# Four-layer network in one kernel: block attention scored by halves, and the routed MLP of four batches moved into the last GLA stages

## What is computed

```python
logits = jnp.einsum('bhtqd,bhtknd->bhtqkn', Qb, Ksel).reshape(Bx, H, Tr, BM, k * BN) * scale
P = jax.nn.softmax(logits, axis=-1)
Ob = jnp.einsum('bhtqs,bhtsd->bhtqd', P, Vsel.reshape(Bx, H, Tr, k * BN, D))
```

```python
top1 = jnp.argmax(gate_probs, axis=-1)
masked = xf[None, :, :] * one_hot.T[:, :, None]
h = jax.nn.relu(jnp.einsum('end,edh->enh', masked, w1) + b1[:, None, :])
expert_out = jnp.einsum('enh,ehd->end', h, w2) + b2[:, None, :]
routing_output = expert_out.sum(axis=0)
shared = jax.nn.relu(xf @ sw1 + sb1) @ sw2 + sb2
return (routing_output + shared).reshape(B, S, D)
```

## Time and profile before

| what | value |
|---|---|
| median of 3 runs | 3938.86 us (3933.8 to 3939.21) |
| the profiled execution's own time | 3959.75 us |
| its span in the profile | 3958.0 us |
| PE, VectorE, ScalarE, GpSimd busy | 3376.5, 2329.6, 1704.5, 528.2 us |
| block attention, from the first exponential of unit 0 to that of unit 31 | 298.6 us |
| GLA stages 14, 15, 16, 17 | 75.17, 63.37, 71.40, 56.80 us |

### The profile page before, as it was taken

One profiled execution on the slowest core, in us unless ns is written; L12 is line 12 of the kernel. 1 busy time (PEld: TensorE's weight loads), 2 busy tenths in 40 slices (PEclk: granted clock), 3 DMA queues, 4 the chain that ended last, 5 costly groups with the idle time before them and its releaser, 6 DMA issues. The chain is left out here.

```text
span 3958.0 us, 124996 instructions
## 1 busy us (share of the span) xinstructions
PE 3376.5 (85%) x55256; PEld 2105.7 (53%) x55256; DVE 2329.6 (59%) x6280; ACT 1704.5 (43%) x3930; POOL 528.2 (13%) x532
## 2 busy tenths in 40 slices
PE   3875665689999999999886996999999999999985
PEld 1334553235555545555564443666666666666672
DVE  3766664267767667676882113666666656666545
ACT  1666774364444444344211434443434444434323
POOL 0212331000000000000000001222222222222210
PEclk9897777789989889898665997999999999999967
DMA  2000000221111111110000001000000000000000
GB/s 90 0 0 1 2 2 3 79 67 40 45 42 46 40 32 53 34 45 29 3 3 18 0 5 41 2 3 2 3 2 3 3 2 3 3 2 2 3 2 24
DMA packets 37036, 77.17 MB, mean 19 GB/s; under 512 B 7696, under 2 KB 11152, under 8 KB 35472
## 3 DMA queue, kind: packets, MB, share of 16 engines
q1 hardware_dynamic: 36496, 69.17, 5.5%
HBM read 64.83 MB, written 4.33 MB: 17 GB/s over the span
## 5 line engine op out<-in xcount | busy, mean ns | idle before, releaser
L1401 PE MATMUL ps<-g_hs,g_fc 128*128 128x512 f32 x448 | 271.6, 691 | 53.2 <-DVE g_hs L1715 37.9
L1523 ACT ACTIVATE g_hidden<-ps 128x512 f32<-128x512 f32 x224 | 133.1, 594 | 409.1 <-PE ps L1401 409.0
L1292 PEld LDWEIGHTS ps<-g_Q,g_K 32*32 32x32 f32 x12288 | 204.5, 120 | 182.3 <-issue 95.6
L2168 PE MATMUL ps<-d_hp,d_w_k 128*128 128x512 f32 x512 | 282.1, 637 | 0.0
L1292 PE MATMUL ps<-g_Q,g_K 32*32 32x32 f32 (+1 forms) x12288 | 235.7, 226 | 27.7 <-DVE g_H L1561 10.0
L1415 PE MATMUL ps<-g_hidden,g_proj 128*128 128x512 f32 x448 | 257.3, 662 | 0.0
L2246 POOL TENSOR_TENSOR d_sq<-d_QK 128x512 f32<-128x512 f32 x128 | 133.0, 1039 | 925.1 <-ACT d_QK L2297 763.8
L2266 ACT ACTIVATE d_F<-ps 128x128 f32<-128x128 f32 x256 | 70.8, 276 | 351.3 <-PE ps L2077 348.0
L778 ACT ACTIVATE att_p<-ps,att_mx 128x96 f32<-128x96 f32 x512 | 165.9, 361 | 70.1 <-DVE att_mx L723 64.5
L1260 POOL COPY g_xb<-X 128x512 f32<-128x512 f32 x8 | 7.2, 906 | 1209.8 <-DVE X L1721 1098.5
L2441 DVE SCALAR_TENSOR_TENSOR d_conv<-ps,w_conv_q,d_conv 128x511 f32<-128x511 f32 (+2 forms) x192 | 142.2, 741 | 33.9 <-ACT d_conv L2291 30.0
(11 more groups left out here) (478 smaller groups left out, 7895.1 us busy)
## 6 DMA issues: line engine op xcount, KB each, us to landing
g_hs<-gate_rows SPq DMA_DIRECT2D x56, 256.0 KB, 3.4
g_fc<-in_c_fc_dram SPq DMA_DIRECT2D x56, 256.0 KB, 4.0
g_proj<-in_c_proj_dram SPq DMA_DIRECT2D x56, 256.0 KB, 2.8
X<-in_x_dram SPq DMA_DIRECT2D x1, 2048.0 KB, 10.7
w_c_fc<-in_c_fc_dram SPq DMA_DIRECT2D x1, 2048.0 KB, 8.3
w_c_proj<-in_c_proj_dram SPq DMA_DIRECT2D x1, 2048.0 KB, 12.7
ex_root<-gate_rows SPq DMA_DIRECT2D x1, 2048.0 KB, 15.2
h_rows<-k SPq DMA_DIRECT2D x1, 2048.0 KB, 6.3
```

Source lines behind the costliest of these rows:

```text
L1292: ins = e.matmul(later(scored, n_), keys_, queries(n_, planes, r_, 4 * i + j), start=(turn_ == 0 and part == 0 and n_ != 1), stop=(part == 1),
L1401: e.matmul(P[2], fc[:, n % 2, ts(f, C)], hs[:, n % 2], start=True, stop=True).then_inc(pe.steps, pe.did(now(f"u{i}")))
L1523: e.activation(r[:, slot], P[2], ACT.Relu).then_inc(act.steps, act.did(now(f"r{i}")))
L2168: ins = e.matmul(b, w_k[:, j, ts(H, C)], hp_of(u)[:, j:j + T], start=(j == 0), stop=(j == TAPS - 1))
```

## The change

In the attention, `scores` and `maximum` get a half as a second argument. Scores of half 0 (banks 0 and 1, row groups 0 and 1) wait for ScalarE's exponentials of half 0 of the unit before instead of for all of them, and `maximum` of half 0 moves on VectorE ahead of `pick_heads(n - 1)` and of `weigh(n, 1)`. The PE issues both halves at the place where it issued the 16 matmuls.

In `gla`, stages 14 to 17 get `routed` = 0 to 3. There the pieces `up`, `down` and `residual` carry the routed MLP of batch 0 to 3, in buffers of the expert MLP. Its weights come by six transfers on SP at the end of stage 13. `up` 0, 1 and 3 are centre, mean and score, `up` 4 to 15 the 12 up matmuls, `down` 3 to 14 the 12 down matmuls. VectorE gets pieces `up` 2 (two instructions) and `up` 3 (two), and two in `residual`. `routed_mlp` then does batches 4 to 7. Three small weights are loaded at the start of the program, and not ahead of `routed_mlp`.

```diff
@@ block_attention
-                        e.wait_ge(pe.steps, pe.at(f"s{last_of(q - RING)}"))
+                        e.wait_ge(pe.steps, pe.at(f"s{last_of(q - RING)}1"))
...
-                def maximum(n):
+                def maximum(n, half):
                     if n >= 2:
-                        e.wait_ge(act.steps, act.at(f"exp{n - 2}3"))
-                    e.wait_ge(pe.steps, pe.at(f"s{n}"))
-                    for half in range(2):
-                        m4 = mx[:, n % 2, ts(half, 8)].rearrange("p (g n) -> p g n", g=2)
-                        e.tensor_reduce(m4, scored[:, ts(half, 2)], AX.X, ALU.max, negate=True).then_inc(dve.steps, dve.did(f"max{n}{half}"))
+                        e.wait_ge(act.steps, act.at(f"exp{n - 2}{2 * half + 1}"))
+                    e.wait_ge(pe.steps, pe.at(f"s{n}{half}"))
+                    m4 = mx[:, n % 2, ts(half, 8)].rearrange("p (g n) -> p g n", g=2)
+                    e.tensor_reduce(m4, scored[:, ts(half, 2)], AX.X, ALU.max, negate=True).then_inc(dve.steps, dve.did(f"max{n}{half}"))
...
                     weigh(n, 0)
+                    if n + 1 < UNITS:
+                        maximum(n + 1, 0)
                     if n:
                         pick_heads(n - 1)
                     weigh(n, 1)
                     if n + 1 < UNITS:
-                        maximum(n + 1)
+                        maximum(n + 1, 1)
                         keep_values(n + 1)
...
-                def scores(n):
+                def scores(n, half):
                     q, u = place_of(n)
                     e.wait_ge(dve.steps, dve.at(f"q{q}"))
                     if n:
-                        e.wait_ge(act.steps, act.at(f"exp{n - 1}3"))
+                        e.wait_ge(act.steps, act.at(f"exp{n - 1}{2 * half + 1}"))
                     for b in range(4):
-                        for g in range(4):
+                        for g in (2 * half, 2 * half + 1):
...
                     if n + 1 < UNITS:
-                        scores(n + 1)
+                        scores(n + 1, 0)
+                        scores(n + 1, 1)
@@ gla
+        routed_h, hidden_rows, masked = hx, r[:, 0:3], r[:, 3:5]
+        routed_up = {2: fc[:, 0], 0: fc[:, 1], 1: hs[:, 0]}
+        routed_down = {2: proj[:, 0], 0: proj[:, 1], 1: hs[:, 1].rearrange("p (f x) -> p f x", f=4)}
+        FEED = (2, 0, 1)
...
+            routed = n - 2 * (B - 1) if half is None and sg is not None else None
...
+                        if c["routed"] == 0:
+                            e.wait_ge(dve.steps, dve.at(was("residual")))
+                            for p_ in FEED:
+                                e.dma_start(routed_up[p_], a["w1_2"][:, p_, :]).then_inc(dma.steps, dma.did())
+                                e.dma_start(routed_down[p_], a["w2_2"][:, p_]).then_inc(dma.steps, dma.did(now("routed")))
...
+                    def routed_step(i):
...
+                        elif i == 3:
+                            e.wait_ge(dve.steps, dve.at(now("rh")))
+                            e.matmul(P[3], routed_gate[:], routed_h[:], start=True, stop=True).then_inc(pe.steps, pe.did(now("rscore")))
+                        elif i >= 4:
+                            x = i - 4
+                            p_, f = FEED[x // 4], x % 4
...
+                            if x:
+                                e.wait_ge(act.steps, act.at(now(f"rr{x - 1}")))
+                            if p_ < 2:
+                                e.wait_ge(dve.steps, dve.at(now(f"rm{p_}")))
+                            moving = routed_h[:] if p_ == 2 else masked[:, p_]
+                            e.matmul(P[2], routed_up[p_][:, ts(f, C)], moving, start=True, stop=True).then_inc(pe.steps, pe.did(now(f"ru{x}")))
+                    def routed_total(x):
...
+                        e.wait_ge(act.steps, act.at(now(f"rr{x}")))
+                        e.matmul(P[3], routed_down[FEED[x // 4]][:, x % 4, :], hidden_rows[:, x % 3], start=(x == 0), stop=(x == 11)).then_inc(pe.steps, pe.did(now(f"rd{x}")))
@@ routed_mlp
-        order = [(b, p_, f) for b in range(B) for p_ in (2, 0, 1) for f in range(4)]
+        order = [(b, p_, f) for b in range(B_LEFT) for p_ in (2, 0, 1) for f in range(4)]
@@ build
-                routed_mlp(k)
+                routed_mlp(k, 4)
```

More of the change, by code:

```diff
@@ L117 @@
 GROUPS = {
-    "all": ["center", "mean", "ident"],
+    "all": ["center", "mean", "ident", "gate_w2", "b1_2", "b2_2"],
     "modulation": ["cT", "wmod"],
@@ L751, in _ @@
                 gather_queries(0)
-                maximum(0)
+                maximum(0, 0)
+                maximum(0, 1)
                 keep_values(0)
@@ L1217, in in_turn @@
                     has = {"copy": c["copy_g"] is not None, "turn": c["tg"] is not None, "make": c["mg"] is not None, "out": c["ob"] is not None,
-                           **{what: c["half"] is not None for what in MLP}}
+                           **{what: c["half"] is not None or c["routed"] is not None for what in MLP}}
                     for what, which in ORDER:
@@ L1392, in up @@
+                    def routed_total(x):
+                        if not 0 <= x < 12:
+                            return
+                        if x == 0:
+                            e.wait_ge(dve.steps, dve.at(now("rm1")))
+                        e.wait_ge(act.steps, act.at(now(f"rr{x}")))
+                        e.matmul(P[3], routed_down[FEED[x // 4]][:, x % 4, :], hidden_rows[:, x % 3], start=(x == 0), stop=(x == 11)).then_inc(pe.steps, pe.did(now(f"rd{x}")))
                     def up(i):
+                        if c["routed"] is not None:
+                            return routed_step(i)
@@ L1403, in down @@
                     def down(i):
+                        if c["routed"] is not None:
+                            return routed_total(i - 3)
                         if c["half"] == 0 and (i < 0 or i >= 12):
@@ L1717, in residual @@
                     def residual(_):
-                        if c["half"]:
+                        if c["routed"] is not None:
+                            x, total = k.X[:, c["routed"], :], hidden_rows[:, 0]
+                            e.wait_ge(pe.steps, pe.at(now("rd11")))
+                            e.tensor_scalar(total, P[3], routed_bias[:, 0:1], None, ALU.add).then_inc(dve.steps, dve.did())
+                            e.wait_ge(dve.steps, dve.n)
+                            e.scalar_tensor_tensor(x, total, m(c["routed"], 2, GB), x, ALU.mult, ALU.add).then_inc(dve.steps, dve.did(now("residual")))
+                        elif c["half"]:
                             e.wait_ge(pe.steps, pe.at(now("d15")))
@@ L1721, in residual @@
                             e.scalar_tensor_tensor(x, P[3], m(c["eb"], 1, GB), x, ALU.mult, ALU.add).then_inc(dve.steps, dve.did(now("residual")))
-                    in_turn(sums=sums, states=states, make=make, turn=turn, out=out, root=root, residual=residual)
+                    in_turn(sums=sums, states=states, make=make, turn=turn, out=out, up=up, root=root, residual=residual)
             k.end(k.slots)
@@ L1737, in gla, with routed_mlp @@
         units()
-def routed_mlp(k):
+def routed_mlp(k, before):
     nc = k.nc
+    B_LEFT = B - before
     with ExitStack() as s:
@@ L1857, in _ @@
                 masks(0)
-                for b in range(1, B):
+                for b in range(1, B_LEFT):
                     norm(b)
@@ L1862, in _ @@
                     masks(b)
-                out(B - 2)
-                out(B - 1)
+                out(B_LEFT - 2)
+                out(B_LEFT - 1)
         k.end()
```

68 lines of the change are left out of this document (59 added, 9 removed).

## The result

| | before | changed |
|---|---|---|
| median, 14 runs each | 3939.61 us (3926.48 to 3958.58) | 3969.88 us (3949.73 to 3986.93) |
| span of the profiled execution | 3958.0 us | 3985.2 us |
| attention, first exponential of unit 0 to that of unit 31 | 298.5 us | 377.2 us |
| GLA stages 14 to 17 | 75.2, 63.4, 71.4, 56.8 us | 86.2, 76.2, 87.1, 74.1 us |
| routed block, first to last up matmul | 181.5 us | 87.9 us |

The ratio is 1.0071, 95% interval 1.005 to 1.0092: 0.7% slower. The three stretches changed by +78.7, +56.9 and -93.6 us. They add up to +42 us where the spans differ by 27. Most of the rest lies outside what the edits work on: GLA stages 2 to 13 took 1001 us in one execution and 991 in the other, and from the end of stage 17 to the first up matmul of the routed block it was 34.2 and 30.6 us.

The account below looks back on a forecast made before the run. Attention was taken as bound by a loop of waits through several engines, the routed block by matmuls. GLA -92 + 47 = -45 us and attention +66 gave +21, median 3960 us (chance 0.60); range 3915 to 4003.

Parts of the forecast that it names:

- The loop in the attention: Attention: VectorE, GpSimd, PE, VectorE wait in a ring; a unit takes 10.25 us at full clock, 12.7 at half, against 9.63.
- I take two thirds: Attention: assumed share of units at half clock, giving 15 + 2/3 x 76 = +66 us.
- The first leg: Attention unit, first reciprocal to second: division, GpSimd, transposes, half-0 scores, maximum and picking; 5.72 us at full clock.
- The second, from the second division to the copy: Attention unit: GpSimd again, four transposes, value transposes and hand-over before keep_values; 2.7 us at full clock.
- The third, copy and gather: End of an attention unit: 2.05 us with keys, 1.65 with queries, 1.85 as a mean.
- less some 8 us because stages 16 and 17 lack the `make` pieces: GLA stages: discount on 50 + 5 us, as stages 16 and 17 have more idle PE to fill; leaves 47 us.
- the two sorts: GLA stages 14 to 17: first sort (14, 16) grows 8.9 us each, second (15, 17) 16.0; 49.8 us together.
- The routed score's wait: GLA stages 14 to 17: PE's score matmul waits for VectorE's two normalizing instructions, 1.3 us four times, 5 us.
- rival 1: Attention: half the matmuls take half the time, loop 9.7 or 11.7 us, total 3936 us; chance 0.13.
- The second (the clock stays up): Attention: full clock all through makes the kernel faster, +15 - 45 = -30 us, total 3909 us; chance 0.14.
- The third (the loop does not bind and the edit does what it suggests): Attention: ScalarE's 64.5 us wait for the maxima goes as well, -110 us, total 3829 us; chance 0.04.
- The fourth (stages swallow what they save): GLA stages: woven matmuls cost 0.427 us an instruction, so that edit gives nothing; +66 us, total 4005 us; chance 0.09.

Follow-up runs that it names:

- e3: Changed kernel with pick_heads(n - 1) moved back in front of maximum(n + 1, 0) on VectorE: 3927.94 us, ratio 0.9946 to the kernel before, attention 326.8 us.
- e10: Changed kernel with half-0 scores first on PE, picking before the first maximum, value transposes directly behind half-1 scores: 3836.96 us, ratio 0.9738, attention 246.9 us.
- e2: GLA edit alone, block_attention as in the kernel before: 3896.08 us, ratio 0.988 to the kernel before, stages 14 to 17 312.3 us.
- e7: Changed kernel with the matmuls of scores half 1 and of outputs done twice: 3958.87 us, ratio 1.0024 to the kernel before, attention 354.2 us.
- e9: Changed kernel with scores(n + 1, 0) moved to the head of the unit on PE: 3863.0 us, ratio 0.9787 to the kernel before, attention 262.8 us.
- e4: Changed kernel with both maxima behind the second division, weigh(n, 1), on VectorE: 3914.83 us, ratio 0.9921 to the kernel before, attention 314.5 us.

## Why the prediction was right, and where it was off

It said slower, 3960 us and +21 us; it measured 3970 and +30. The mechanism held step by step; in the attention two legs of the loop were undersized, and elsewhere errors cancelled.

**The loop in the attention** was forecast from two queues, and each piece was then seen. Scores of half 0 to the maximum were put at 1.28 and 2.17 us and measured 1.25 us at full clock and 2.14 in most units at half. The picking on the loop, 1.55 us, is what e3 took off. `keep_values` waiting for the value transposes is the 59.7 us in the waits view, and the wait that e10 removed. The signs named beforehand came true: attention between 330 and 390 us, VectorE's wait for the scores its largest at 109.6 us (over 60 was named), the clock at 0.64 (0.67 was named). A half's instructions at 1.1 us were seen in e10, since in the changed kernel the two halves run into each other.

**The sizes in the loop.** The attention grew by 79 us where 66 was forecast. "I take two thirds" was the chosen share of half clock; the mean clock of 0.64 is a share of 0.72 to 0.73, and 15 + 0.73 x 76 = 70 us. The other 9 us show when each unit is cut at its first division, its second and its copy. The first leg came out at 6.66 us in the mean of the 28 units that gather, where its two sums, 5.72 and 7.19 us, give 6.70 at two thirds. The second, from the second division to the copy, was put at 2.7 us at full clock and 3.67 at half. It took 3.68 us in 26 of 31 units and 3.51 in three more, even where the scores ran at full clock, because the value transposes, behind the PE's long wait for the division, ran at half clock nearly every time. That is 0.3 us a unit more than a share of two thirds gives. The third, copy and gather, was put at 1.85 us and took 2.08: 1.66 with queries, but 2.44 with keys and not 2.05. So one share for the whole loop was the weak term, and the gather of keys the other.

**The stages.** Forecast +47 us, measured +57 in the profile of the changed kernel and +46 in that of e2. The stage lengths forecast, 86, 78, 80 and 70 us, stand against 84, 75, 82 and 72 in e2: two too long and two too short, so that the sum agrees better than its parts. The step "less some 8 us because stages 16 and 17 lack the `make` pieces" isn't borne out. In e2 these two grew by 10.3 and 15.3 us, as much as the 8.9 and 16.0 of the two sorts without any discount; what fell short was stage 15, with 11.3 us for 16. The routed score's wait was put at 1.3 us on top of the old 2.17 us; it was about 4 us in all where it was seen, of the size expected.

**The routed block** was forecast to lose 92 us and lost 93.6.

**Luck.** By medians the attention edit alone costs 74 us (66 forecast) and the GLA edit alone gives 53 (45 forecast). Each is off by 8 us, in opposite directions, so their sum of about +20 us hits the forecast of +21 more closely than either part does. The changed kernel's own +30 us is within the noise of that sum.

**Slips in the recorded sums.** The range's upper end, +65 us, doesn't follow from its terms: -92 + 55 + 91 is +54. In rival 1, "+46 - 20 = about +42" doesn't add up; its two loops at a share of two thirds give +39 us for the attention, so 3933 us and not 3936. Neither changes the forecast.

**The rivals.** The first (half the matmuls take half the time) fell with the 1.13 and 2.03 us. The second (the clock stays up) fell in the direction, 0.64 instead of 0.79, but e7 shows that the time it set on the clock was there to be had, as far as a rise to 0.80 can show it. The third (the loop does not bind and the edit does what it suggests) fell with the waits view; e9, by moving one call, comes some way to it, with 36 us less than before where the rival says 64.5. The fourth (stages swallow what they save) fell with e2.

## What to carry to other kernels

When a wait is split so that work may start earlier, look where the work stands in the queue of its engine: here the scores were free to go and stood behind transposes that needed two other engines, and moving the call to the head of the queue turned +0.7% into -2.1% (with the GLA edit in both), and the attention from 377 into 263 us. On an engine that works in order, an instruction that waits must not stand in front of work that is ready, or the second becomes part of the first one's loop. Splitting a group of matmuls by row groups of the array halved the work of each part and not its time (1.13 us against 1.15).

## What the runs showed that I had not expected

Adding work made the kernel faster, which the prediction had no place for: 1472 PE instructions more in the attention, 23 us less (377 to 354), with the granted clock up from 0.64 to 0.80. And a better order on PE is paid twice, since the clock rose along with it, from 0.64 to 0.83 in e9 and 0.88 in e10. A shorter loop alone didn't do that: e3 and e4, which change only VectorE's order, cut 50 and 63 us and stayed at 0.65 and 0.62. In the changed kernel the ring of waits costs its own time, and the PE is at 1.2 GHz for 0.73 of it on top.
